# One stage of a decoder kernel rewritten: expert rows combined on TensorE, the q/k/v projection by 512-token groups in f16 parts

## The reference, cut to what matters

```python
# end of _L0_ffn_ref: 4 expert rows a token, each times its gate
yrows = ye[eid, posc] * gflat[:, None]
out = yrows.reshape(-1, K, D).sum(axis=1)
out = out + jax.nn.silu(X @ sw1.T) * (X @ sw3.T) @ sw2.T
# the residual and the normalization between the two
x = _layernorm(x + ffn)
# start of _L1_attn_ref; Wq 256x1024, Wk and Wv 256x256
q, k, v = x @ Wq, x @ Wk, x @ Wv
q, k = rope(q), rope(k)      # x1*cos - x2*sin, x1*sin + x2*cos
```

## Time and profile before

| | |
|---|---|
| median of 3 runs | 3371.53 us (3366.98 to 3377.83) |
| the profiled execution | 3378.72 us, its span 3376.7 us |
| mean granted TensorE clock | 0.869 |
| PE, PEld busy | 2539.4 us (75%), 1410.9 us (42%) |
| DVE, ACT, POOL busy | 1873.9 us (55%), 1415.8 us (42%), 1078.8 us (32%) |
| stage `l1p` | from 960.2 to 1181.8 us |

### The profile page before, as it was taken

One profiled execution on the slowest core, in us unless ns is written; L12 is line 12 of the kernel. 1 busy time (PEld: TensorE's weight loads), 2 busy tenths in 40 slices (PEclk: granted clock), 3 DMA queues, 4 the chain that ended last, 5 costly groups with the idle time before them and its releaser, 6 DMA issues. The chain is left out here.

```text
span 3376.7 us, 43990 instructions
## 1 busy us (share of the span) xinstructions
PE 2539.4 (75%) x15362; PEld 1410.9 (42%) x15362; DVE 1873.9 (55%) x4985; ACT 1415.8 (42%) x2858; POOL 1078.8 (32%) x852
## 2 busy tenths in 40 slices
PE   6978886685635688788874689696777788768776
PEld 3323334464422333333362266473443233355555
DVE  4476665465658555555422467144431777564687
ACT  4334451463421256666602434224412355546754
POOL 1045561146355366566602300001001211102355
PEclk9979998797867889999986779897697799968988
DMA  3222201620454311111002210201001322014022
GB/s 108 72 47 47 46 3 35 201 71 19 125 167 83 97 48 40 44 44 30 16 13 65 41 30 1 109 4 29 14 0 42 66 35 28 3 46 119 1 96 80
DMA packets 185737, 182.84 MB, mean 54 GB/s; under 512 B 55161, under 2 KB 152186, under 8 KB 184750
## 3 DMA queue, kind: packets, MB, share of 16 engines
q1 hardware_dynamic: 176110, 167.48, 17.6%
q0 software_dynamic: 9408, 12.56, 2.4%
HBM read 121.81 MB, written 61.59 MB: 54 GB/s over the span
## 5 line engine op out<-in xcount | busy, mean ns | idle before, releaser
L929 POOL TENSOR_TENSOR l1a_p_lo<-res,l1a_p_hi 128x1024 f16<-128x1024 f32 x192 | 311.8, 1643 | 178.4 <-ACT res L1170 178.4
L1179 ACT ACTIVATE l0a_probs<-ps 128x1024 f32<-128x1024 f32 (+1 forms) x192 | 145.6, 810 | 175.4 <-PE ps L1033 103.1
L1179 ACT ACTIVATE l3a_probs<-ps 128x1024 f32<-128x1024 f32 (+1 forms) x192 | 146.9, 809 | 143.7 <-PE ps L1033 116.2
L1169 ACT ACTIVATE l1a_p_hi<-ps 128x1024 f16<-128x1024 f32 x192 | 157.9, 822 | 112.4 <-PE ps L1033 81.8
L1030 PE MATMUL ps<-l1a_qs,l1a_ks 128*128 128x512 f16 (+3 forms) x768 | 167.4, 332 | 32.2 <-ACT res L1170 32.2
L1201 DVE CUSTOM_DVE_ANT_0 l1a_masked<-ps,l1a_wide_mask 128x128 bf16<-128x128 f32 (+3 forms) x256 | 118.1, 490 | 103.3 <-PE ps L999 101.0
L954 POOL TENSOR_TENSOR l0a_both<-l0a_probs 128x768 f32<-128x768 f32 (+2 forms) x96 | 154.7, 1633 | 46.2 <-PE ps L1071 46.0
L999 PE MATMUL ps<-l1a_ks,l1a_qs 128*128 128x512 f16 (+3 forms) x384 | 121.9, 347 | 62.0 <-DVE l1a_nmax L1204 33.2
L2750 PE MATMUL ps<-x_m,x_x 128*128 128x462 f16 (+1 forms) x672 | 140.6, 359 | 31.1 <-PEq L111 30.5
L1170 ACT ACTIVATE res<-ps 128x1024 f32<-128x1024 f32 x192 | 158.1, 824 | 0.0
L1033 PE MATMUL ps<-mask_t,ident_b 128*128 128x128 bf16 x768 | 157.6, 225 | 0.0
(11 more groups left out here) (733 smaller groups left out, 6501.1 us busy)
## 6 DMA issues: line engine op xcount, KB each, us to landing
f_wf<-in_L_ffn_w_dram SPq DMA_DIRECT2D x16, 1024.0 KB
f_slots<-x0a_zeros SPq DMA_DIRECT2D x32, 256.0 KB
f_xe<-f_slots SPq DMA_DIRECT2D x32, 256.0 KB, 3.1
f_ys<-f_y SPq DMA_DIRECT2D x32, 256.0 KB
l1a_qs<-l_q_h SPq DMA_DIRECT2D x64, 128.0 KB
d_wall<-in_L_ffn_W_dram SPq DMA_DIRECT2D x3, 2112.0 KB
l0a_qs<-l_q_h SPq DMA_DIRECT2D x32, 128.0 KB
l0a_ks<-l_k_h SPq DMA_DIRECT2D x16, 256.0 KB
```

The source lines that it names most:

```text
L929: pool.tensor_tensor(ph_lo[:, n % SLOTS, :, 0:w], probs[:, n % FULL, :, 0:w], ph_hi[:, n % SLOTS, :, 0:w], ALU.subtract).then_inc(s_["low_ ...
L1169: act.activation(ph_hi[:, n % SLOTS, :, 0:w], SB[n % 2][:, :, 0:w], ACT.Exp)
L1179: act.activation(probs[0:KR, n % SLOTS, 2 * pr:2 * pr + 2, 0:w], SB[x % 2][:, :, 0:w], ACT.Exp).then_inc(s_["exps"], 1)
```

## The change

`project_in` loses its rotary branch, `Combine` keeps only its tiles, and a new function runs the stage by groups of 512 tokens, 5 pairs (4 of q, 1 of k) in each, 20 in all. Its parts:

- The gates become 128x128 diagonals, written by ScalarE, and TensorE sums in PSUM: an identity times `acc`, then 4 diagonals times the gathered rows, all f32. The residual is added to `acc` for all groups at the start. Mean, variance and scaling read PSUM. There are 20 gather buffers.
- The weights and the normalized columns are split into two f16 parts, and each product is three f16 terms (high by high, high by low, low by high).
- PSUM slots, `tmp`, `st` and the parts hold two pairs of 2 x 512; `tmp` lies in `k.xtr`. GpSimd issues 5, 4, 4 and 3 gathers for the next group ahead of the sums of pairs 0 to 3. Each pair is stored by 4 DMAs of 128 rows of 512.

```diff
-                for n, j in enumerate(firsts):
-                    if ahead and b == 0 and n < 4:
-                        ahead.gather(pool, 32 + 8 * n, 40 + 8 * n)
-                    pool.wait_ge(ph.s["mults"], 3 * (b * R + n) + 3)
...
+    GS = 20
+    GATHERS = (5, 4, 4, 3, 0)
+    TERMS = [(0, 0), (0, 1), (1, 0)]
...
+            for n, (g, p) in enumerate(pairs):
+                if g == 2 and p == 0:
+                    for i in range(2):
+                        sp.wait_ge(stored[i], 64 * PAIRS)
+                    early.queries(sp)
+                    early.keys(sp)
+                sp.wait_ge(s_["lo_done"], n + 1)
...
+            gather(0, EACH)
+            for n, (g, p) in enumerate(pairs):
+                if g + 1 < NG:
+                    at = (g + 1) * EACH + sum(GATHERS[:p])
+                    gather(at, at + GATHERS[p])
+                pool.wait_ge(s_["mults"], n + 1)
+                if n >= 2:
+                    pool.wait_ge(s_["lo_done"], n - 1)
+                t = tmp[:, n % 2]
+                pool.tensor_tensor(st[:, n % 2, 0, :], t[:, 0, :], t[:, 2, :], ALU.subtract).then_inc(s_["rotated"], 1)
+                pool.tensor_tensor(st[:, n % 2, 1, :], t[:, 1, :], t[:, 3, :], ALU.add).then_inc(s_["rotated"], 1)
...
+            def summed(t):
...
+                pe.matmul(C[:, t % GT, :], k.ident[:], combine.acc[:, t, :], start=True, stop=False)
+                pe.wait_ge(s_["diag"], (t + 1) * K0)
+                for j in range(K0):
+                    i = t * K0 + j
+                    pe.wait_ge(g_ld[i % GS], 16 * (i // GS + 1))
+                    ins = pe.matmul(C[:, t % GT, :], dg[:, i % EACH, :], yg[:, i % GS, :], start=False, stop=j == K0 - 1)
+                ins.then_inc(s_["combined"], 1)
...
+            for n, (g, p) in enumerate(pairs):
+                project(n)
+                if p == 0:
+                    rows(g)
+                if g + 1 < NG:
+                    for t in {1: (0,), 2: (1,), 3: (2, 3)}.get(p, ()):
+                        summed((g + 1) * GT + t)
+                    if p == PAIRS - 1:
+                        columns(g + 1)
...
+            for n, (g, p) in enumerate(pairs):
+                if p == PAIRS - 1 and g + 1 < NG:
+                    roots(g + 1)
+                if p == 1:
+                    rows(g)
+                upper(n)
+                if g + 1 < NG and p < GT:
+                    diagonals((g + 1) * EACH + p * K0, (g + 1) * EACH + (p + 1) * K0)
+                if p == PAIRS - 1 and g + 1 < NG:
+                    columns(g + 1)
...
+            for n, (g, p) in enumerate(pairs):
+                last = p == PAIRS - 1
+                rotate(n)
+                if n and p:
+                    lower(n - 1)
+                if g + 1 < NG and p == PAIRS - 2:
+                    moments(g + 1, 0)
+                if last and g + 1 < NG:
+                    moments(g + 1, 1)
+                    variances(g + 1)
+                    normal(g + 1)
+                if last:
+                    lower(n)
+                if last and g + 1 < NG:
+                    columns(g + 1)
```

More of the change, by code:

```diff
@@ L1768, in _ @@
                         pe.wait_ge(ph.s["kept"], b * len(keeps) + job.needs)
-                    if ahead and j == 0:
-                        for g in (0, 1) if b == 0 else ():
-                            ahead.columns(pe, g)
-                        pe.wait_ge(ahead.s["xts_ready"], 2 * b + 2)
                     for c0, w, terms in job.parts(b):
@@ L1776, in _ @@
                     ins.then_inc(ph.s["jobs_done"], 1)
-                    if ahead and b == 0 and j in (5, 9):
-                        ahead.columns(pe, 2 if j == 5 else 3)
         @block.scalar
         def _(act):
-            for g in (0, 1) if ahead else ():
-                ahead.roots(act, g)
-                ahead.moved(act, g)
             act.wait_ge(ph.s["w_ld"], 16 * len(loads))
@@ L1787, in _ @@
                 for j, job in enumerate(jobs):
-                    if job.kind in ("first", "second"):
-                        if job.kind == "second":
-                            for half in range(2):
-                                r = b * R + firsts.index(j - 1)
-                                act.wait_ge(ph.s["rotated"], 2 * r + half + 1)
-                                after(act, ph.s["rstored"], 16 * 2 * job.n_dst * r)
-                                act.activation(his[:, half, :], st[:, half, :], ACT.Copy).then_inc(ph.s["hi_done"], 1)
-                        if ahead and b == 0 and j in (3, 7):
-                            ahead.roots(act, 2 + j // 4)
-                        if ahead and b == 0 and j in (5, 9):
-                            ahead.moved(act, 2 + j // 8)
-                        continue
                     act.wait_ge(ph.s["jobs_done"], b * NJ + j + 1)
@@ L1863, in _ @@
+            if split:
+                for b in range(B):
+                    for n, j in enumerate(stores):
+                        dve.wait_ge(ph.s["staged"], b * len(stores) + n + 1)
+                        lower(b * len(stores) + n, j % 2)
         @block.gpsimd
         def _(pool):
-            if not R:
-                if early:
-                    early.fill(pool)
-                return
-            if ahead:
-                ahead.gather(pool, 0, 32)
-            for b in range(B):
-                for n, j in enumerate(firsts):
-                    if ahead and b == 0 and n < 4:
-                        ahead.gather(pool, 32 + 8 * n, 40 + 8 * n)
-                    pool.wait_ge(ph.s["mults"], 3 * (b * R + n) + 3)
-                    after(pool, ph.s["lo_done"], 2 * (b * R + n))
-                    pool.tensor_tensor(st[:, 0, :], tmp[:, 0, :], tmp[:, 2, :], ALU.subtract).then_inc(ph.s["rotated"], 1)
-                    pool.tensor_tensor(st[:, 1, :], tmp[:, 1, :], tmp[:, 3, :], ALU.add).then_inc(ph.s["rotated"], 1)
-                if early and b == 0:
-                    pool.wait_ge(ph.s["rotated"], 2 * R)
-                    early.fill(pool)
+            if early:
+                early.fill(pool)
```

315 lines of the change are left out of this document (178 added, 137 removed).

## The result

The changed kernel takes 3392.5 us (median of 5 runs, 3388.2 to 3399.1) against 3371.5 for the kernel before (5 runs): a ratio of 1.0061, 95% interval 1.0045 to 1.0077. It is slower by 21 us, where 3369 and no change were predicted; the value lies half a microsecond above the range of 3346 to 3392. The profiled execution took 3390.94 us, its span 3389.1.

What follows compares the result with a forecast made beforehand. VectorE was full from 1016 to 1100, then no engine; the new groups were GpSimd's work plus a chain through all engines. Stage end 1179.1, not 1181.75, gave 3376.1; less 7.2 for the profiled execution, 3369 us, range 3346 to 3392.

Steps and rivals of the forecast that it cites:

- the price of the stores: Stage's end: four store issues 2.4 us, 2.7 from last issue to next stage; earlier stores fit in the two-pair buffers.
- the tail: Last pair's sums to next stage: sums 2.3, high part 1.0, low part 1.2, stores and landing; 9.7 us.
- The last group: Its first sums to its last sums, with no gathers left: 17.6 us, last sums starting at 1169.4.
- To the first sums: Stage start to first rotary sum: sixteenth gather's landing at 984.3, then 15.7 us of work, so sums start at 1000.0.
- The periods: One group's first sums to the next's, three times: GpSimd's gathers and sums 21.7 us plus chain 28.9, 50.6 each.
- The chain from the fourth pair's sums: Group's end through all engines to the next group's sums: 23.1 us at 2.4 GHz, 31.2 at 1.2, 28.9 taken.
- The sign that the prediction named for it: If right, GpSimd would be idle by 20 us or more at each group's end.
- Both links that the prediction named in the chain: Group's end: fourth tile's diagonals (1.1 us) behind the high part; fifth pair's projection (2.8 or 5.5) behind gate products.
- The halfway value for gate products and fifth pair: In the chain, TensorE's clock halfway for gate products (1.8 to 3.5 us) and fifth pair's projection (2.8 to 5.5).
- A (full clock): Rival, chance 0.20: TensorE stays at 2.4 GHz, the group-end chain takes 23.1 us, the kernel 3352 us.
- B (TensorE the bound): Rival, chance 0.18: TensorE bounds the groups below mean clock 0.67; kernel 3413 us at 1.2 GHz, 3391 halfway.
- C: Rival, chance 0.05: groups overlap fully, GpSimd alone sets 33.1 us a group, stage 55 us early, kernel 3316 us.

Runs made afterwards that it cites:

- the third chip: The changed kernel profiled again without edit on another chip: 1.0067 of the kernel before, stage 235.8 us.
- two such moves: Changed kernel with one-head stores, fourth tile's diagonals made with the third's, fifth pair's projection ahead of the last two tiles' gate products: 0.9964.
- early high parts: On top of one-head stores and both queue moves, SyncE issues high-part stores without waiting for the low part: 0.9960.

## Why the prediction was wrong

**The step that failed is the price of the stores.** The prediction took "four store DMAs at 0.61 ... 2.4, and 2.7 from the last issue's end to the next stage", and said that the pairs' stores "fit in two of" the buffers. Both rested on the earlier trace rows, rows of the old stores of 32 rows, or of loads of 64 rows; the price of the issues was right (2.5 us for the four), but that of the landing was carried over to a pattern that no row of before has. It measured 8.1 us for 2.7, and a wait of 2.6 us for a buffer ahead of the last high part, and the sums took 3.5 for 2.3, since a low part stood beside them: 9.2 of the tail's 9.3 us. The last group (2.3 too long) and the third period (4.2) hold waits of the same kind. Mending the stores alone brought 1.0061 to 1.0023, and the tail to 12.8; halving the outermost dimension brought 1.0237. With stores of 32 rows the landing took 2.8 us, as predicted; what the tail still had over 9.7 were the sums (3.5) and eight issues of 0.46 where four of 0.61 were counted.

The rule is in the Trainium skill, page "DMA: Bandwidth & Descriptors", section "Why a DMA increments its semaphore by 16 and not by 1": a DMA runs on as many engines as the largest number up to 16 that divides the slowest dimension of both its sides. The traces agree for 4 entries (share 0.27, a quarter) and for 2 (0.14, an eighth). For 32 the page gives all 16 engines; the mean share of 0.50 lies in a stretch where SyncE issues a store every 0.46 us, and its single slices reach eight tenths. The runs have 2, 4 and 32 entries; what the rule says of other numbers no run here shows.

**To the first sums**: 39.8 predicted, 42.8 here, 41.1 to 42.8 in the other traces. The chain behind the last gather was right: 14.5 us from the last gate product's end to the sums, where 14.8 were predicted (15.7 less the product's 0.9). But that product started 27.1 us into the stage and not 24.1. Of the 3 us, 2.5 are GpSimd's: it issued the sixteenth gather 23.1 us into the stage, 20.6 before, since four of its first seven issues took 1.4 to 2.0 us where the others took 1.0. All four lie beside VectorE's additions for the residual or its subtractions for the weights, which take two SBUF inputs, and the third chip's trace has the same; no run takes these away. The prediction had called the splitting of the weights hidden by the gathers.

**The periods**: 50.6 predicted, 52.1 and 52.5 measured here, 51.4 and 51.3 on the third chip. The chain from the fourth pair's sums took 28.2 and 29.4 us for 28.9; most of the excess lies in GpSimd's part ahead of it, 23.9 and 23.2 us for 21.7. The mechanism was the one described: TensorE waited 29.6 us for diagonals in 11 waits, GpSimd was idle for 13 us twice at the third period's end, the products after a pause ran at 1.2 GHz (5.30 us for twelve). The sign that the prediction named for it, GpSimd idle by 20 us or more at each group's end, did not fit its own sum, which leaves 17: it was 12.4, 16.4 and, with no gathers left, 26.6. Both links that the prediction named in the chain were tested by taking them out, and both paid. The halfway value for gate products and fifth pair, 6.8 us, was near the 6.1 measured (granted clock 0.53 in the gate products, 3.4 us, and 1.00 in the pair straight behind them, 2.75). By the rule cited from the Trainium skill, page "TensorE: Matmul & The Clock Gate", section "HAM oscillation — how this bites in real kernels", a burst behind such a wait starts cold. This one did, and so did the transposes (0.50) and the projection behind them. The prediction read more out of the rule, that every product of the chain runs at 1.2 GHz; the fifth pair did not.

**The last group** without store waits took 17.1 us, for 17.6 predicted. Of the multiplications beside GpSimd's sums, where the prediction had no row, the run with one-head stores has these:

```profile
1160.56 1.21 DVE L2057 TENSOR_TENSOR l1p_los<-l1p_st,l1p_his 128x1024 f16<-128x1024 f32 x1
1160.71 2.18 POOL L1901 TENSOR_TENSOR l1p_st<-res 128x512 f32<-128x512 f32 x1 [1.35 <-DVE res L2052]
...
1162.85 1.27 POOL L1902 TENSOR_TENSOR l1p_st<-res 128x512 f32<-128x512 f32 x1
1162.89 0.68 DVE L2051 TENSOR_TENSOR res<-ps,l1p_sin 128x512 f32<-128x512 f32 x1
```

Beside a low part, which reads two SBUF tiles, the sum takes 2.18 and not 1.27; beside a multiplication, which reads PSUM and a table, neither is longer. Both halves of the rule that the prediction cited from the Trainium skill, page "SBUF — State Buffer", section "Who interferes with whom", hold here.

**The rivals.** A (full clock) did not come: 0.84, 0.80 and 0.78. B (TensorE the bound) gave a time near the one measured, 3391 at its lower end, but by luck, for a reason that did not occur: TensorE was busy 32 to 35 us of 52 to 55 and the clock stayed above the 0.67 from which it decides. C did not come. Without the tail, the last group's waits and the third period's excess over its neighbours, 22.2 - 9.3 - 2.3 - 2.5 leaves 8.1 us of error in a stage of 241, 3 of them up to the first sums.

## What to carry to other kernels

A store or load is priced by its pattern, not by its bytes: look at the outermost dimension of both sides. By the Trainium skill's rule cited above it should be a multiple of 16, of which the runs show 32; where it is not, cut the transfer so that it is, even if that takes more DMAs. Smaller DMAs alone don't help: as many and as small ones with 2 outermost entries gave 1.0237, with 32 they gave 1.0023. When a buffer of two is freed by a store, the slow store shows first as a wait of the engine that fills it, far from the DMA, and again in full at the barrier. And where one engine's queue interleaves two groups' work, put what the other engines wait for longest ahead, whatever its place in the program: two such moves, which add no instruction, and the mended stores turned a loss of 0.7% into a gain of 0.4% on the same chip. With the early high parts and the added products it is 0.9951, not told apart from that.

## What the hardware showed that I had not expected

The rate of a store halves with its outermost dimension: 91 GB/s at a share of 0.27 with 4 entries, 48 at 0.14 with 2, and 127 at 0.50 with 32, each measured in the tail, where almost nothing else moves. And 50 products of no use a group bring the clock of a chain from about 0.8 to between 0.90 and 1.00. They cost nothing while they fall into TensorE's waits (in the old chain the transposes started 0.1 us behind the scaling), and 1.0 to 2.1 us a period where the wait is shorter than they are; in sum they still made no period longer than the same chain without them.
